# A recurrent block with a product-key expert layer: more MLP items beside time mixing, one receptance unit per step, four staging buffers for MLP stores, and down projections placed anew beside the experts

## The reference, cut to what matters

```python
xn = layernorm(x)
# time mixing (attn)
xk, xv, xr = (xn * tm + shifted(xn) * (1 - tm) for tm in (time_mix_k, time_mix_v, time_mix_r))
k, v = xk @ Wk.T, xv @ Wv.T
sr = sigmoid(xr @ Wr.T)                      # "receptance"
rwkv = sr * wkv(-exp(time_decay), time_first, k, v)   # a scan over the 2048 tokens
s = rwkv @ Wo.T
# ffn: experts and MLP
sim = einsum(xn @ Wq.T, keys)                # 4 heads x 2 halves x 128 keys
scores, indices = the 8 best of 8 x 8 pairs of the 8 best of each half   # 32 experts a token
w = silu(einsum(xn, down_embed[indices])) * softmax(scores)
experts = einsum(w, up_embed[indices])       # rows of two 16384 x 1024 tables
mlp = (silu(xn @ Wg.T) * (xn @ Wu.T)) @ Wd.T # 4096 wide
out = x + s * silu(mlp + experts)
```

## Time and profile before

| | |
|---|---|
| median of 3 runs | 2066.27 us (2027.64 to 2077.34) |
| the profiled execution | 2049.32 us |
| its span, slowest core | 2047.8 us (other cores 2018.8 to 2046.9) |
| TensorE busy | 1329.8 us, 65% |
| VectorE (DVE) busy | 1246.2 us, 61% |
| ScalarE (ACT) busy | 901.0 us, 44% |
| GpSimd (POOL) busy | 851.0 us, 42% |
| DMA | 607.94 MB, mean 297 GB/s |
| granted TensorE clock, mean | 0.861 on core 3 |

### The profile page before, as it was taken

One profiled execution on the slowest core, in us unless ns is written; L12 is line 12 of the kernel. 1 busy time (PEld: TensorE's weight loads), 2 busy tenths in 40 slices (PEclk: granted clock), 3 DMA queues, 4 the chain that ended last, 5 costly groups with the idle time before them and its releaser, 6 DMA issues.

```text
span 2047.8 us, 23272 instructions; the slowest of 8 cores (2018.8 to 2047.8 us)
## 1 busy us (share of the span) xinstructions
PE 1329.8 (65%) x5504; PEld 551.4 (27%) x5504; DVE 1246.2 (61%) x2531; ACT 901.0 (44%) x1480; POOL 851.0 (42%) x776
## 2 busy tenths in 40 slices
PE   1278648866686668776788356556665656756787
PEld 0133223322232223332333112222222222222333
DVE  3838885888668884874444235555655555655555
ACT  3634314332343333444554265544554444554444
POOL 0033333343333333341333224656555556564562
PEclk9999888987897889887899667878887788887899
DMA  8899999999999999977986897999999999999996
GB/s 267 261 314 294 301 305 306 312 301 302 301 305 309 312 309 320 307 254 246 307 274 215 288 294 256 324 316 315 312 319 303 322 320 317 315 310 300 308 323 213
DMA packets 229111, 607.94 MB, mean 297 GB/s; under 512 B 37872, under 2 KB 70640, under 8 KB 226928
## 3 DMA queue, kind: packets, MB, share of 16 engines
q0 software_dynamic: 73888, 268.73, 41.6%
q1 hardware_dynamic: 91008, 268.48, 41.2%
q10 hardware_dynamic: 64080, 69.24, 11.8%
HBM read 510.15 MB, written 96.47 MB: 296 GB/s over the span
## 4 chain that ended last, share of the span: by engine, by line
DMA 36%; DVE 23%; PE 20%; issue 12%; ACT 4%; POOL 3%; DVEq 1%; ACTq 0%; another core or an unknown queue 0%; SPq 0%; POOLq 0%
DMA arena<-tabb,expi 20%; DMA h_scr<-arena 9%; PE ps_d L436 4%; DVE arena L628 3%; POOL arena L419 3%; PE ps_b L436 3%; PE ps_c L436 3%; DMA arena<-x_nat 3%; DMA arena<-wdT 2%; DVE arena L684 2%; DVE arena L682 2%; PE ps_b L571 2%; PE ps_a L571 2%; PE ps_d L571 2%; DVE arena L688 2%
## 5 line engine op out<-in xcount | busy, mean ns | idle before, releaser
L419 POOL DMA_INDIRECT arena<-tabb,expi x512 | 555.6, 1085 | 585.9 <-PE ps_a L571 173.4
L1083 ACT ACTIVATE arena<-arena 128x1024 bf16<-128x1024 bf16 x384 | 404.3, 1053 | 405.6 <-DVE arena L898 358.4
L405 POOL CAST arena<-arena 128x1024 bf16<-128x1024 f32 x256 | 293.6, 1147 | 584.8 <-DMA arena<-downE 343.2
L898 DVE TENSOR_TENSOR arena<-arena 128x1024 bf16<-128x1024 bf16 x384 | 262.5, 692 | 358.8 <-DMA arena<-tabb,expi 224.7
L436 PE MATMUL ps_b<-arena 128*128 128x512 bf16 x1024 | 261.0, 400 | 48.1 <-ACT arena L1005 45.2
L436 PE MATMUL ps_c<-arena 128*128 128x512 bf16 x1024 | 250.5, 388 | 9.3 <-DVE arena L806 9.3
L806 DVE TENSOR_TENSOR arena<-arena,ps_c 128x512 bf16<-128x512 bf16 x128 | 85.7, 681 | 271.8 <-DMA h_scr<-arena 97.9
L436 PE MATMUL ps_a<-arena 128*128 128x512 bf16 x512 | 148.0, 445 | 152.4 <-ACT efac L988 100.4
L571 PE MATMUL ps_a<-arena 128*128 128x512 bf16 x384 | 115.2, 456 | 134.1 <-DVE arena L859 128.5
L571 PE MATMUL ps_b<-arena 128*128 128x512 bf16 x320 | 101.0, 473 | 130.8 <-DVE arena L859 121.5
L1005 ACT ACTIVATE arena<-ps_b 128x512 bf16<-128x512 f32 x128 | 74.8, 597 | 235.0 <-PE ps_b L436 175.4
(11 more groups left out here) (99 smaller groups left out, 1577.9 us busy)
## 6 DMA issues: line engine op xcount, KB each, us to landing
arena<-downE SPq DMA_DIRECT2D x128, 512.0 KB, 10.5
arena<-upE SPq DMA_DIRECT2D x128, 512.0 KB, 10.4
tabb<-arena SPq DMA_DIRECT2D x256, 256.0 KB, 8.9
arena<-x_nat SPq DMA_DIRECT2D x32, 512.0 KB, 6.8
arena<-wgS ACTq DMA_DIRECT2D x32, 512.0 KB
arena<-wuS ACTq DMA_DIRECT2D x32, 512.0 KB
h_scr<-arena ACTq DMA_DIRECT2D x64, 256.0 KB
arena<-wdT SPq DMA_DIRECT2D x32, 512.0 KB
```

Source lines behind the costliest of these rows:

```text
L405: e.tensor_copy(out=tout[s], in_=ring[s]).then_inc(pool_cast, 1)
L419: e.indirect_dma_start(out=gslot[n % NSLOT], out_offset=None, in_=d_tabb, in_offset=IndirectOffsetOnAxis(ap=expi[:, n:n + 1], axis=0)).the ...
L898: e.tensor_tensor(out=pdot[q % 3], in0=gslot[slot][:, 0:1024], in1=xnl[w % 2], op=ALU.mult).then_inc(dv_prod, 1)
L1083: e.activation(out=pdot[q % 3], in_=pdot[q % 3], func=AF.Copy, accum_out=dots[:, g * GS + x:g * GS + x + 1]).then_inc(ac_dots, 1)
```

## The change

- `NI1` is 56 in place of 48: `items(u)` puts 1, 2, 2, 2 items in turn in the steps of time mixing, and window 0 alone holds the last 8.
- `h1s` has four buffers with a semaphore each. The room comes from the receptance: `sr` has two buffers in place of eight. Some buffers of the first and the last stretch lie elsewhere for it (`pre_st`, `xt[3]`).
- The block of 8 receptance units becomes `r_unit(u + 1)` at the end of each step on TensorE, all in `ps_x[0]`, and its sigmoid `receptance(u + 1)` at the end of each step on ScalarE. `sims` now waits for `ac_sr`. The mix for r moves from step m = 3 to m = 7 of a block, behind the first `hidden` of the step.
- The down projections are set by `wd_tiles`: tiles 0, 1, 2 in windows 2, 3, 4; tiles 3 and 4 in window 5; 5, 6, 7 in windows 6, 7, 8; 8 and 9 in window 9; from window 10 on the window's own tile, ahead of its experts in PSUM.
- The second half of the Wd chunks and Wo are cast in window 1, three in a group, in place of window 2, four in a group. SyncE loads x tile 3 behind its wait for the MLP stores.

```diff
-NI1 = 48
+NI1 = 56
...
-    sr_m = [b16(A_SR + m * 1024, 512) for m in range(KC)]
+    sr = [b16(A_SR + i * 1024, 512) for i in range(2)]
...
-    h1s = [b16(A_H1S + i * 2048, 1024) for i in range(2)]
+    h1s = [b16(A_H1S + i * 2048, 1024) for i in range(4)]
...
     def items(u):
-        return range(u * 3 // 2, (u + 1) * 3 // 2)
+        return range(u * 7 // 4, (u + 1) * 7 // 4)
+
+    wd_tiles = {2: (0,), 3: (1,), 4: (2,), 5: (3, 4), 6: (5,), 7: (6,), 8: (7,), 9: (8, 9)}
+    for w in range(10, NT):
+        wd_tiles[w] = (w,)

     def quantum(w, g):
+        tiles = wd_tiles.get(w, ())
+        if len(tiles) == 1:
+            t, = tiles
             lo = (0, 5, 10, 16, 21, 26, 32, 32, 32)
+            go = 6 - max(0, 2 * (w - t - 1))
+            return [(t, range(lo[g], lo[g + 1]), range(4 * (g - go), 4 * (g - go + 1)) if g in (go, go + 1) else ())]
...
     def sync_prog(e):
...
-        load_xt(3)
...
-        for i in range(2):
-            e.wait_ge(st_h1[i], 16 * 32)
+        for i in range(4):
+            e.wait_ge(st_h1[i], 16 * 16)
+        load_xt(3)
         load_h1(0)
...
     def tensor_prog(e):
...
+        def r_unit(u):
+            b, m = u // KC, u % KC
+            e.wait_ge(ac_pre, n_wr(m))
             e.wait_ge(dv_mixr, b + 1)
+            if u == 0:
+                e.wait_ge(ac_xfm, NT)
+            elif u % 2:
+                e.wait_ge(dv_sx, u // 2 + 1)
             else:
+                e.wait_ge(ac_sr, u)
+            unit(ps_x[0], wr_m[m], lambda kc: mix_r[:, ts(kc, TB)]).then_inc(pe_r, 1)
...
             gu_unit(its[0], 0)
-            if m % 2:
-                gu_unit(its[0], 1)
             if m == 0:
-                r_units(b)
                 q_units(b)
             if m % 2 == 0:
                 sims(4 * b + m // 2)
+            if len(its) == 2:
+                gu_unit(its[0], 1)
             if u + 2 < NU:
                 k_unit(u + 2)
-            if m % 2:
+            if len(its) == 2:
                 gu_unit(its[1], 0)
             if u + 1 < NU:
                 v_unit(u + 1)
             gu_unit(its[-1], 1)
+            if u + 1 < NU:
+                r_unit(u + 1)
...
         def hidden(n):
...
-                if i >= 2:
-                    e.wait_ge(st_h1[i % 2], 16 * (i // 2))
+                if i >= 4:
+                    e.wait_ge(st_h1[i % 4], 16 * (i // 4))
...
+            if m == 7 and b + 1 < NB:
+                e.wait_ge(pe_r, KC * (b + 1))
+                mix(mix_r, 16, b + 1, dv_mixr)
+            for n in units[1:]:
+                hidden(n)
...
     def scalar_prog(e):
...
+        def receptance(u):
+            e.wait_ge(pe_r, u + 1)
+            if u >= 2:
+                e.wait_ge(dv_rwkv, u - 1)
+            e.activation(out=sr[u % 2], in_=ps_x[0], func=AF.Sigmoid).then_inc(ac_sr, 1)
...
                 gate(2 * i + 1)
+            if u + 1 < NU:
+                receptance(u + 1)
...
-                elif w == 2 and g < 6:
+                elif w == 1:
                     if g == 0:
                         store_h1(2 * NIC - 1)
-                    for c in range(16 + 4 * g, 20 + 4 * g):
+                    for c in range(16 + 3 * g, 19 + 3 * g):
                         cast_d(c)
```

More of the change, by code:

```diff
@@ new lines, in quantum @@
+        if len(tiles) == 2:
+            t = tiles[0]
+            lo = (0, 11, 22, 32)
+            if g < 3:
+                return [(t, range(lo[g], lo[g + 1]), ())]
+            if g == 3:
+                return [(t, (), range(KC)), (t + 1, range(0, 8), ())]
+            if g < 7:
+                return [(t + 1, range(8 * (g - 3), 8 * (g - 2)), ())]
+            return [(t + 1, (), range(KC))]
+        return []
+    def finished(w, g):
+        tiles = wd_tiles.get(w, ())
+        if len(tiles) == 1 and w - tiles[0] == 2 and g == 7:
+            return tiles[0]
+        if len(tiles) == 2 and g == 5:
+            return tiles[0]
+        before = wd_tiles.get(w - 1, ())
+        if before and g == 1 and w - 1 - before[-1] < 2:
+            return before[-1]
@@ L824, in vector_prog @@
             its = items(u)
-            hidden(2 * its[0])
-            if m % 2:
-                hidden(2 * its[0] + 1)
-                next(pairs)
-                hidden(2 * its[1])
-                next(pairs)
-                if b + 1 < NB and m == 3:
-                    mix(mix_r, 16, b + 1, dv_mixr)
-            else:
-                best_keys(t)
-            hidden(2 * its[-1] + 1)
+            units = [2 * i + j for i in its for j in range(2)]
+            hidden(units[0])
+            if m % 2 == 0:
+                best_keys(t)
+            if m == 7 and b + 1 < NB:
[3 more added lines that the diff above has]
+                hidden(n)
+                if m % 2:
+                    next(pairs, None)
             if m % 2:
@@ L1030, in scalar_prog @@
             if m == 0:
-                for i in range(KC):
-                    e.wait_ge(pe_r, KC * b + i + 1)
-                    e.wait_ge(ac_pre, NW0)
-                    if b:
-                        e.wait_ge(dv_rwkv, KC * (b - 1) + i + 1)
-                    e.activation(out=sr_m[i], in_=ps_x[i % 2], func=AF.Sigmoid).then_inc(ac_sr, 1)
                 for j in range(4):
```

107 lines of the change are left out of this document (38 added, 69 removed).

## The result

The changed kernel takes 1953.63 us as the median of 4 runs (1950.62 to 1989.53), the kernel before 2051.05 us in the same comparison (4 runs, 2027.64 to 2077.34). The ratio is 0.961, 95% interval 0.956 to 0.966. It leaves out the runs in a slower state, more than 1.5% above the fastest of their kernel (2077.34 and 2066.27 before; 1989.53 after, where four cores had a granted clock of 0.77), so it isn't the quotient of the medians. Measured again beside other kernels it was 0.955 (0.953 to 0.958) and 0.953 (0.950 to 0.956). The forecast was faster, 0.976; the gain is more than one and a half times that. As a ratio, 0.961 lies at the inner edge of the stated 0.960 to 0.992, and the two later ones lie outside it.

What follows compares the result with a forecast made beforehand. DMA was taken to bound the large stretches, and the chain of steps to end time mixing. 926 + 97 + 108 + 867.5 us, plus 1.5, gave 2000 us, ratio 0.976, or 2016 as a median; range 1984 to 2050.

Steps and rivals of the forecast that it cites:

- What bounds the kernel: Large stretches are bound by DMA; the steps end time mixing some 55 us after the table, so the seam holds the gain.
- Parts 1 to 3: Steps of time mixing: buffers gain 55 us, receptance 48 less 22, eight items cost 18; steps end at 877, not 940.
- the new wait on ScalarE: End of each step: ScalarE waits for the receptance unit; 0.7 us a step stays uncovered, 22 us in all.
- Part 4: End of the expert table: at 306 GB/s it moves from 886 to 918 us; first product at 926, 19 us won.
- The added term: Bytes moved ahead of the table's end, 6.3 MB of items and 3.6 of steps, delay it from 886 to 918 us.
- Part 5: Windows 0 to 2: window 0 takes 97 us, window 1 with the casts 108, and window 2 becomes a normal 61.3.
- Part 6: Down projections: double windows cost 5 us each; two leave the end, two come in windows 5 and 9; net 0.
- ScalarE didn't become the chain: Slower rival, chance 0.06: 5.9 us uncovered in each of 32 steps, steps end at 1044; median 2131 us.
- the seam didn't give it back: Rival, chance 0.12: casts stretch window 1 to 122 us and middle double windows cost 10 each; median 2044 us.
- The rival of the table not slowed: Chance 0.14: the table's ring holds its rate, first gather at 888 us, product at 896; 1970 us, median 1986.
- The rival of the late steps: Chance 0.16: steps still end time mixing near 940 us, table hidden, window 0 takes 88; median 2026 us.

Runs made afterwards that it cites:

- e12: Kernel before, plus 32 DRAM-to-DRAM copies (16.8 MB) issued by GpSimd ahead of the first gather; ratio 1.021.
- e9: The changed kernel again, unedited, timed and traced in a later comparison; ratio 0.955 to the kernel before.
- e2: Changed kernel with items, casts and down projections as before, so only the four buffers and the receptance unit per step are left; ratio 0.969.
- e3: Changed kernel with the down projections back in the old order; ratio 0.959.
- e4: Changed kernel with 48 items in the steps, 16 in windows 0 and 1 and the casts in window 2, as before; ratio 0.966.
- e1: The kernel before, unedited, for a second trace; mean span 21.5 us shorter than in the execution the prediction was made on.
- e6: Changed kernel with two buffers for MLP stores again in place of four; ratio 0.964.
- e11: Changed kernel plus 32 DRAM-to-DRAM copies (16.8 MB) issued by GpSimd ahead of the first gather; ratio 1.001.
- e13: Changed kernel plus 16.8 MB as 64 plain loads into spare SBUF from GpSimd's queue, each after the last landed; ratio 0.981.
- e14: Changed kernel with the down projections in the old order, the same edit as e3, timed beside the changed kernel; ratio 0.962.
- e15: The changed kernel again, unedited, timed beside e14; ratio 0.953.
- e10: Changed kernel with the pairs of down projections in windows 2 and 3 rather than 5 and 9; ratio 0.955.
- e7: Changed kernel with each MLP store made twice, the second to a tensor nobody reads; steps 105 us slower, last table cast at 883 us.

## Why the prediction was right and where it was wrong

**What bounds the kernel: right.** The steps set the end of time mixing in the kernel before, 58 us behind its own table, and the gain was to be found at the seam. e12 shows it: 115 us more of table cost 38.

**Parts 1 to 3, the steps: right in sum.** They were to end at 877 us; they ended at 871, and at 875 in e9. The terms: buffers 55, measured 40 to 46; the receptance 48 - 22 = 26 net, measured 44 to 50; the items 18, measured 26 to 32 (e2 to e3 and e4 to e9). So the errors of the terms cancel in part, and the sum came out closer than they did. If the 48 us were right, the new wait on ScalarE cost next to nothing rather than 22. No run separates the two, but ScalarE still waits 54.3 us for DVE, so there was slack to cover it.

**The table loads.** The view of line 1029 in the changed kernel, durations as least, median and most, then first and last start:

```profile
L1029 ACT ACT_TABLE_LOAD  x32: 1283/1283/1283, 121.0 to 849.8; - x32
L1029 ACT ACTIVATE arena<-ps_d x32: 597/597/597, 122.3 to 851.1; 128x512 bf16<-128x512 f32 x32
```

Each sigmoid starts 1.3 us after its load does, at the first step as at the last. Ahead of a load there is no gap either where ScalarE has work; the timeline of ACT, same core:

```profile
855.76 0.63 ACT L1001 ACTIVATE arena<-arena 128x512 f32<-128x512 f32 x1
...
856.40 1.28 ACT L1011 ACT_TABLE_LOAD   x1
857.70 1.09 ACT L1011 ACTIVATE arena<-ps_b 128x512 bf16<-128x512 f32 x2
```

The Trainium skill ("ScalarE: Activation LUTs", "What ACT_TABLE_LOAD costs") adds 1380 ns of drain to a switch; the load's 1283 ns agree, the drain isn't seen here either: 440 of the 784 loads of the eight cores start less than 0.1 us after the activation ahead of them.

**Part 4, the table's end: the step that failed.** The prediction had the last cast near 912 us, the first gather at 918 and the first product at 926. They came at 889, 893 and 903 as means, and at 895, 899 and 910.5 on the slowest core. What failed is the rate: core 3's 306 GB/s from 96 to 886 us, its last cast at 881, was carried on as the kernel's. That was one core in one execution. The eight cores had their last cast between 842 and 881, and in the kernel before the difference was hidden, since all eight waited for their steps until 936 to 950. In e1 the same core had it at 843. In the changed kernel core 3 moved the 251.6 MB that the prediction gave it, but at 317 GB/s:

```profile
96.00:889.00 793.00, 642.47 (x2859) 272.67 (x2856) 630.57 (x1460) 361.49 (x478) 294.26 (x256) 0.93 1.01 317
```

From 96 us to the last cast the mean over the cores was 312 GB/s before and 316 after, and 319 and 321 in e1 and e9. The prediction's 251.6 MB at 321 GB/s end at 880 us, at 316 at 892; e9 has 874 and the first trace 889.

The added term was nearly right, in part by luck. It was 32 us for 9.9 MB. The mean moved by 31.6 us (857.5 to 889.1), but for 12.6 MB, as the rate rose too; from e1 to e9 it was 38.1 us for 13.3 MB.

So the first product moved by 44.5 us on the mean, and by 50 from e1 to e9, and not by 19. The mean span fell by 94.7 us, and by 96.1 from e1 to e9 (89.7 to 91.7 over the runs of two comparisons), against the forecast's 49.3; by the means this step is 26 to 31 us of what is missing. Told by the slowest cores, which the prediction followed, 46 us are missing (1952.5 for 1998.5): 15.5 in the first product, 12.8 in windows 3 to 14 (722.8 for core 3's 735.6, again a slow core's base), 8.9 in the last window, and the rest in windows 0 to 2.

**Part 5, windows 0 to 2: too dear by 10 to 13 us.** Windows 1 and 2 together went from 195.1 to 156.0, and from 195.0 to 152.4 in e1 and e9; the prediction had 198.9 to 169.3. Window 1 was 102 to 104 rather than 108, and window 2 is not a normal window of 61.3: 51 to 52. By the traces of all cores it starts with 12 gathers issued, a normal one with 9, and it gives these back in its course; that the casts in window 1 hold up DVE and ScalarE but not GpSimd is my reading of why, and wasn't tested. Window 0 was right within some 4 us.

**Part 6, the down projections: right to some 10 us.** Windows 5 and 9 took 64 and 66, as costed. The last window lost 9.6 us, beyond the bound of 8 that the prediction gave and then left out of its sum; windows 3 to 14 gained or lost 4 to 6 us against the kernel before. Net, 4 to 14 us were won where the prediction had 0.

**The rivals.** The steps didn't end late, ScalarE didn't become the chain, and the seam didn't give it back (window 1 at 102 to 104, not 122; the double windows 3 to 7 us over the others, not 10). The rival of the table not slowed comes nearest in time (1986) but by another cause: the table was slowed by what the bytes say, from a base 24 to 45 us lower. The rival of the late steps is what e6 is: steps at 921, the table hidden, and window 0 at 88.4, where that rival had 88.

## What to carry to other kernels

A wait that is hidden on every core can differ between cores and executions by more than the change under study; before a hidden chain is made the visible one, take its length from all cores and from a second trace. Once it is visible, the core with the latest chain tends to set the time: in the first trace of the changed kernel and in those of e3, e4, e9, e11, e13, e14 and e15 the slowest core is the one whose table ended last (in e10 it isn't, nor in e1, where the table is hidden). When two chains run side by side, here 870 us of steps and a table of 889, count both: e6 gives up 46 us of the steps and loses 30 us of the span. Where the DMA engines are full, price moved work in bytes at the stretch's own rate. That was right within 3 us for the loads of e13 (56 us for 53), 6 us short from e1 to e9, and far short for copies within DRAM (94 for 53).

## What the runs showed of the hardware

An issue of a DMA isn't always cheap for its engine: with each MLP store made twice on ScalarE's queue (e7) the issues grew from 0.35 to 0.38 us to as much as 10.8, and the steps lost 105 us. This happened in a stretch where the DMA engines were at 1.02 and the stores had packets of 512 bytes. SyncE's issues in the same stretch (core 3, 96 to 850 us) stayed at a median of 0.38 us and at most 1.5, so it was the one queue.

A copy from DRAM to DRAM moved the table's end by 5.6 us a MB (e11; 6.8 in e12), a load of the same bytes by 3.3 (e13). Window 0 is 10 to 14 us shorter where its 16 gathers are issued before it starts: it takes 112.4 us in e12 (11 issued, as a mean) against 98.9 in e1 (16), and 98.5 in e9 (10) against 88.4 in e6 (16). That the gathers are the whole reason wasn't tested by itself.
